# Two chunks of eight fetched by TensorE instead of one, and edge fields held in SBUF, in a graph network kernel on one Trainium2 core

## What is computed

```python
# L0, two layers: weighted messages
msg = h[src] * edge_weight[:, None]
h_neigh = segment_sum(msg, dst) * inv_deg
# L1, two layers: messages with per-edge attributes
m = (h * norm_out)[src] * (mu + exp(ls) * edge_attr)
agg = segment_sum(m, dst) * norm_in @ W + b
# L2, two layers: attention over 5 heads
e = leaky_relu(xl[src] + xr[dst]); alpha = einsum('ehc,hc->eh', e, att)
out = segment_sum(softmax_by_dst(alpha)[:, :, None] * xl[src], dst)
# L3, two layers: attention over 4 heads with 8 edge types
alpha = leaky_relu(qn[etype, dst] + kn[etype, src])
agg = segment_sum(softmax_by_dst(alpha)[:, :, None] * xw[etype, src], dst)
```

## Time and profile before

| | us |
|---|---|
| median of three runs (11,395.51 to 11,404.53) | 11,397.69 |
| the profiled execution | 11,410.16 |
| its span, first to last instruction | 11,408.1 |
| busy: DVE, PE, POOL, PEld, ACT | 6,968.2, 6,336.2, 5,957.6, 4,385.4, 1,664.8 |

### The profile page before, as it was taken

The page is one execution under the profiler, slowest core; times in us unless marked ns, Lnnn a source line. Parts: engine busy times, 40 slices in busy tenths (PEclk is TensorE's granted clock), DMA queues, the critical chain, the costliest instruction groups (busy, mean ns, idle before and its releaser), DMA issues. The chain is left out here.

```text
span 11408.1 us, 146167 instructions
## 1 busy us (share of the span) xinstructions
PE 6336.2 (56%) x31639; PEld 4385.4 (38%) x31640; DVE 6968.2 (61%) x9723; ACT 1664.8 (15%) x5751; POOL 5957.6 (52%) x6263
## 2 busy tenths in 40 slices
PE   1777777676666764555276455544743332923327
PEld 1555454444444432222166222224732221722226
DVE  6777545577767767777888677778941112711118
ACT  0222344200000001000065100004610000000000
POOL 2777677577767735666200266640007775057760
PEclk8666778666666656666555566665555555855558
DMA  2333444444444426888388388865923333333333
GB/s 66 93 91 92 111 124 126 102 122 120 116 110 122 121 64 209 261 263 263 96 350 333 124 263 262 264 189 216 388 103 87 85 85 67 98 91 85 85 78 105
DMA packets 983109, 1719.05 MB, mean 151 GB/s; under 512 B 527619, under 2 KB 597268, under 8 KB 929127
## 3 DMA queue, kind: packets, MB, share of 16 engines
q1 hardware_dynamic: 577360, 1118.77, 28.7%
q0 software_dynamic: 227424, 434.31, 17.6%
q10 hardware_dynamic: 178256, 165.14, 4.4%
HBM read 1271.04 MB, written 448.16 MB: 151 GB/s over the span
## 5 line engine op out<-in xcount | busy, mean ns | idle before, releaser
L537 POOL DMA_INDIRECT gathered_rows<-node_table,stage x2912 | 2800.0, 962 | 1245.8 <-issue 874.4
L537 POOL DMA_INDIRECT gathered_rows<-xl_table,stage x1664 | 1572.9, 945 | 1916.3 <-DMA stage<-slots 1436.6
L537 POOL DMA_INDIRECT gathered_rows<-rel_table,stage x1664 | 1570.1, 944 | 1908.4 <-DMA stage<-slots 1401.8
L557 PE MATMUL ps_sum<-messages,onehots 128*125 128x65 f32 (+3 forms) x13312 | 2209.2, 339 | 529.2 <-DVE messages L1654 246.3
L557 PEld LDWEIGHTS ps_sum<-messages,onehots 128*125 128x125 f32 x13312 | 2154.3, 254 | 660.8 <-issue 655.3
L680 PE MATMUL ps_G<-table_parts,low_onehots 125*128 125x400 bf16 x4992 | 1551.3, 486 | 818.7 <-DVE low_onehots L691 797.2
L1420 PE MATMUL ps_Z<-xr_parts,onehots_turned 125*128 x4992 | 1293.5, 437 | 1116.1 <-DVE z L1446 1067.3
L698 DVE TENSOR_TENSOR rows_by_feature<-ps_G,high_onehots 128x400 f32<-128x400 f32 x1664 | 944.3, 574 | 1159.0 <-PE ps_G L680 1126.4
L1532 PE MATMUL ps_Q<-query_parts,onehots_turned 125*128 x4992 | 655.3, 205 | 1486.9 <-DMA onehots_turned<-onehots_turned 1484.4
L1420 PEld LDWEIGHTS ps_Z<-xr_parts,onehots_turned 125*128 125x128 bf16 x4992 | 654.4, 131 | 1755.9 <-issue 1350.8
L680 PEld LDWEIGHTS ps_G<-table_parts,low_onehots 125*128 125x128 bf16 x4992 | 587.1, 128 | 1606.0 <-issue 1183.8
(11 more groups left out here) (297 smaller groups left out, 5087.8 us busy)
## 6 DMA issues: line engine op xcount, KB each, us to landing
stash_a<-gathered_rows SPq DMA_DIRECT2D x208, 1300.0 KB
kept_rows<-stash_a SPq DMA_DIRECT2D x208, 1300.0 KB
onehots<-onehots_kept SPq DMA_DIRECT2D x520, 500.0 KB
onehots_turned<-onehots_turned SPq DMA_DIRECT2D x416, 250.0 KB
stash_r<-gathered_rows ACTq DMA_DIRECT2D x208, 272.0 KB
kept_rows<-stash_r SPq DMA_DIRECT2D x208, 272.0 KB
onehots_kept<-onehots ACTq DMA_DIRECT2D x104, 500.0 KB
gathered_rows<-node_table,stage POOLq DMA_INDIRECT x2912
```

Source lines behind the costliest of these rows:

```text
L537: pool.indirect_dma_start(G[:, HALF * k + q, 0:width], None, table, bass.IndirectOffsetOnAxis(stage[:, k, field, q:q + 1], 0)).then_inc(ga ...
L557: return nc.tensor.matmul(ps_sum[0:BN, bass.ds(at, width)], S[:, j, :], M, start=False, stop=True, skip_group_check=True)
```

## The change

Five things are edited.

1. TensorE fetches two chunks of a group, and GpSimd gathers six. The table is split by the block number into a part within five (`fifth`) and a part that is summed: for each fetched chunk five one-hots (one for each position `a` in a set of five blocks) are multiplied with five tables of 64 x 5 columns, and the 15 matmuls (five times three bf16 parts) of 320 columns add up in one PSUM bank. VectorE makes ten one-hots of 128 columns in one instruction of 1,280, multiplies the bank by a one-hot of five and reduces over five, once per chunk.
2. `slots` and `stage` are gone. `src_all`, `weight_all`, `low_all`, `high_all` and `fifth_all` stay in SBUF until the fourth network needs the space; source-and-type indices and types go to DRAM once and are loaded back as a whole before the relation passes.
3. ScalarE copies the 8 index columns of a group to a small tile (`keep_index`), and in neighbour passes the 8 weight columns, from those tiles.
4. GpSimd waits itself for the slot to be free and for `keep_index`, where it waited for `stage`.
5. At the start, `types` is written with one long row per partition, where `slots` was written in pieces of 256 B; VectorE computes `fifth` and the row of the low index.

```diff
-WIDE = 16
-BANKS = D // WIDE
+FETCH = 2
+FIVE = 5
...
-        def gather_loop(pool, stage, G, width, table, field, count=HALF):
+        def keep_index(act, IDX, index, i, k):
+            nc.scalar.activation(IDX[:, k, :], index[:, bass.ds(i * U + HALF * k, HALF)], ACT.Copy).then_inc(index_kept.sem, 1)
+        def gather_loop(pool, G, width, table, IDX, free, count=HALF):
             with pool.Fori(0, TURNS) as i:
                 for k in range(K):
-                    pool.wait_ge(staged[k].sem, staged[k].at(16 * i + 16))
+                    free(pool, i, k)
+                    pool.sem_inc(pool_seen, 1)
+                    pool.wait_ge(index_kept.sem, index_kept.at(K * i + k + 1))
...
-            for t in range(BANKS):
-                pe.wait_ge(bank_picked.sem, bank_picked.at(BANKS * n + t - 1))
-                for part in range(3):
-                    last = nc.tensor.matmul(ps_G[:, t % 2, 0:WIDE * NB], OT[0:BN, k, :],
-                                            HP[:, part, WIDE * t:WIDE * (t + 1), :].rearrange("p f b -> p (f b)"),
-                                            start=part == 0, stop=part == 2)
+            for g in range(FETCH):
+                pe.wait_ge(bank_picked.sem, bank_picked.at(FETCH * n + g - 1))
+                for a in range(FIVE):
+                    for part in range(3):
+                        last = nc.tensor.matmul(ps_G[:, (FETCH * k + g) % 2, 0:D * FIVE], OT[0:BN, k, g, a, :],
+                                                HP[:, part, a, :, :].rearrange("p f b -> p (f b)"),
+                                                start=a == 0 and part == 0, stop=a == FIVE - 1 and part == 2)
...
-            v.tensor_scalar(OT[0:BN, k, :], LR[0:BN, k, :], part[0:BN, 0:1], None, ALU.is_equal).then_inc(low_made.sem, 1)
+            v.tensor_tensor(OT[0:BN, k, :, :, :], LR[0:BN, k, :].rearrange("p (g e) -> p g e", e=P).unsqueeze(2).to_broadcast([BN, FETCH, FIVE, P]),
+                            ids[0:BN, 0:FIVE].unsqueeze(1).unsqueeze(3).to_broadcast([BN, FETCH, FIVE, P]), ALU.is_equal).then_inc(low_made.sem, 1)
...
                                 ahead, slot = i + (k + K // 2) // K, (k + K // 2) % K
                                 sp.wait_ge(z_made.sem, z_made.at(4 * (K * i + k - 1)))
                                 sp.sem_inc(sp_seen, 1)
-                                sp.wait_ge(stashed[slot].sem, stashed[slot].at(16 * ahead))
-                                sp.sem_inc(sp_seen, 1)
-                                stage_next(ahead, slot)
+                                load_turned(sp, ST, ahead, slot)
```

More of the change, by code:

```diff
@@ L383, in _ @@
                     link(v.tensor_scalar(low, low, -1.0, None, ALU.add))
-                    link(v.tensor_copy(fin[:, BLOCK, :, :], be[:, 0, :].unsqueeze(2).to_broadcast([P, NT, C])))
+                    fifth = fin[:, SRC_FIFTH, :, :]
+                    link(v.tensor_scalar(fifth, high, float(FIVE), None, ALU.is_ge))
+                    for b in range(2, FIVE):
+                        link(v.scalar_tensor_tensor(fifth, high, float(FIVE * b), fifth, ALU.is_ge, ALU.add))
+                    link(v.scalar_tensor_tensor(over[:, :, :], fifth, -float(FIVE * BN), a_src, ALU.mult, ALU.add))
                     v.scalar_tensor_tensor(fin[:, SRC_TYPE, :, :], fin[:, SRC, :, :], float(R), fin[:, TYPE, :, :],
@@ L489, in build @@
         coef_made = Counted("coefficients_made")
-        staged = [Counted(f"staged_{k}") for k in range(K)]
         gathered = [Counted(f"gathered_{k}") for k in range(K)]
@@ L705, in picks_over @@
                 c.over(16 * TURNS)
-            for c in (low_made, high_made, row_picked):
+            for c in (low_made, high_made):
                 c.over(GROUPS)
-            for c in (bank_made, bank_picked):
-                c.over(BANKS * GROUPS)
+            for c in (bank_made, bank_picked, row_picked):
+                c.over(FETCH * GROUPS)
             table_split.over(1)
@@ L716, in weighted_sums @@
             with es:
-                stage = sb("stage", [P, K, R, HALF], I32, es)
-                stage_f = stage[:, :, :, :].bitcast(F32)
+                IDX = sb("index", [P, K, HALF], I32, es)
+                W = sb("weights", [P, K, HALF], F32, es)
                 G = sb("gathered_rows", [P, U, D], F32, es)
@@ L745, in _ @@
                             for k in range(K):
-                                if hist:
-                                    stage_group(sp, stage, i, k, (stashed[k],))
-                                else:
-                                    stage_group(sp, stage, i, k)
+                                if not hist:
+                                    chunks_free(sp, i, k)
                                     load_onehots(sp, S, i, k)
@@ L756, in _ @@
                     def _(pool):
-                        gather_loop(pool, stage, G, D, node_table, SRC, HALF - 1)
+                        gather_loop(pool, G, D, node_table, IDX, chunks_free, HALF - FETCH)
                     @block.scalar
                     def _(act):
+                        for k in range(K):
+                            keep_index(act, IDX, src_all, 0, k)
                         with act.Fori(0, TURNS) as i:
@@ L941, in _ @@
                         link(v.tensor_copy(ps_c[:, D:2 * D], mu))
-                        split_table(HP, BR[0:BN, :, :])
-                        pick_rows(dve, stage_f, LR, OT, HI, BR, ps_G, G, 0, 0)
+                        make_ids(ids)
+                        split_table(HP, rest[:, :, :, :])
+                        pick_rows(dve, LR, OT, HI, ids, BR, ps_G, G, 0, 0)
                         def turn(i, last_turn):
@@ L1488, in pair_scores, with relation_scores @@
                     c.over(NCH // 2)
+                index_kept.over(GROUPS + K)
                 for c in (mult_made, reduced, scored):
                     c.over(NCH // QD)
-        def relation_scores(SCORE, XQ):
+        def relation_scores(SCORE, XQ, src_type, types):
             phase[0] += 1
@@ L1537, in _ @@
                     def _(act):
+                        for k in range(K):
+                            keep_index(act, IDX, src_type, 0, k)
                         with act.Fori(0, TURNS) as i:
@@ L1713, in build @@
         segments_phase()
+        early.close()
         norm_phase()
@@ L1860, in build, with _ @@
             dense(H[:, :, :], D, [wfc[:, :]], take, None, after)
+        kept_types = sb("kept_types", [P, 2, NS], I32)
+        types_back = sem("types_back")
+        with nc.Block() as block:
+            @block.sync
+            def _(sp):
+                sp.dma_start(kept_types[:, :, :], types_dram).then_inc(types_back, 16)
+                sp.wait_ge(types_back, 16)
         norm_phase()
```

221 lines of the change are left out of this document (123 added, 98 removed).

## The result

The changed kernel takes 11,659.4 us (median; 11,658.1 to 11,661.7) against 11,396.6 us (11,391.8 to 11,404.5) for the kernel before: a ratio of 1.023, 95% interval 1.0212 to 1.0248. The profiled execution has a span of 11,659.9 us, 251.8 more than before; the medians differ by 262.8, because the profiled execution of the kernel before took 13.6 us more than its median and that of the changed kernel 2.3. The prediction was 11,726 us: the sign and the main mechanism hold, and one term of its sum, the gain in the pair passes, was half as large as it should have been.

The account below looks back on a forecast made before the run. It took GpSimd's gathers to bound most passes, a VectorE-TensorE loop the first neighbour and attribute passes, and `stage` waits to slow pair passes. 374 + 212 - 130 - 120 - 8 = +328 us gave 11,726 us, range 11,440 to 11,960.

Parts of the forecast that it names:

- the gain in the pair passes: Pair passes with `stage` gone: between -128 and 0 us per pass, taken as -60, so -120 us for both.
- The loop in three passes: First neighbour and attribute passes: VectorE and TensorE wait for each other in a loop; +212 and +374 us.
- The fixed part: Loop time per group besides the fetch F: 4.7 us in an attribute pass, 5.06 in the first neighbour pass.
- The fetch: TensorE's 30 matmuls per group: 4.35 us at a high clock, 8.1 at a low one, 6.1 expected.
- d: Time into a fetch after which TensorE's clock rises: taken as 3.4 us; the range counted 2.9 to 4.8.
- The second neighbour pass: Loop open there, one-hots ready ahead, so the pass falls to GpSimd's six gathers, 7.49 us per group: -130 us.
- the other reading: Pair passes: DMA engines go round queues packet by packet, so gathers get their share during a store; both passes -256 us.
- second rival: Pair passes at GpSimd's pace, the rest as forecast: 136 us less, 11,590 us; chance 0.12.
- The rest: Start of the kernel and starts of pair and relation passes: -13, +4, +5 and 4 x -1, -8 us.
- The break-even: Where the first rival's outcome changes sign: F + 4.7 near 9.9 us, a fetch of 5.2 us.
- first rival: TensorE's clock stays high in all four neighbour and attribute passes: -218 us, 11,180 us; chance 0.13.
- The rival in which the change doesn't do what it says: Gathers are issued, but their waits, with ScalarE's index copy queued, hold GpSimd; folded into the range, no chance of its own.

Follow-up runs that it names:

- ahead: The changed kernel with VectorE making a group's one-hots one group earlier, same instructions: 10,582 us, 0.9286 of the kernel before (12,737 us on the slow chip).
- hold_clock: The changed kernel with 12 more matmuls per group, useless for the output, in TensorE's pause in the two attribute passes: 11,276 us in one run.
- pair_seven: The changed kernel with seven gathers instead of eight per group in the pair passes, leaving out every eighth chunk's scores: 11,394 us in one run.
- the first four runs: Changed kernel, slow chip: old one-chunk fetch 13,365 us; one chunk by five one-hots 13,209; two chunks only in second neighbour pass 13,133; one-hots a group earlier 12,737.
- run 50: Not a run's number: "that run" is the first measurement of `ahead`, on the slow chip, 12,737 us; 50 counts its late gathers in a pair pass.

## Why the prediction was right, and where it was not

- **The loop in three passes** was the mechanism. `ahead` shows it by opening the loop, `hold_clock` by shortening one term of it. The fixed part was 4.9 us in an attribute pass where the prediction had 4.7: in the group shown the pick starts 0.11 us behind the fetch instead of 0.04, and from the end of the reduce to the next one-hots it is 2.15 us instead of 2.05, with 0.03 in the other links. Attribute passes +383 (forecast +374), first neighbour pass +227 (+212).
- **The fetch**: 1.48 us for the one-hots and 0.49 for a pick came out as the slope of the earlier trace rows gave them. The reduce took 0.49; the forecast has 0.47, where the slope that it names gives 0.50. The fetch at a high clock took 4.25 us against 4.35; the other bound, 8.1, was never reached (the longest took 7.2), so it and its allowance for the last matmul remain untested. The mean fetch of the attribute passes is 6.1 us, as forecast, and in the shown group of 5.92 the clock is low for about the 3.4 us that the prediction chose as d. That choice was a judgment between 2.9 and 4.8, which would have made some 75 us less or 205 more, and in part luck: the reason given for it (no waits for picks) was not tested, and the low stretch does not begin where it was thought to.
- **The second neighbour pass**: -129 us, forecast -130.
- **The pair passes are the step that failed.** From the earlier trace rows (421 GB/s in the store, 201 outside it) the prediction concluded that gathers and stores take turns rather than overlap, and took half of the possible gain, -60 us per pass. It was -126 and -124. What the prediction set beside it as the other reading, that gathers get their share during a store, gives -256; the runs gave -251, with 310 GB/s during the store and 296 behind it. The mean tells it: 7.4 us at 0.74 and 3.2 at 1.08 are a share of 0.84, and the same bytes in 10.0 instead of 11.2 us need no more than 0.94; in the trace after they needed 0.88, 292 GB/s. The burst of 421 GB/s followed a long stretch at 201, so it shows what the engines can carry, not that a group's bytes need all of it. `pair_seven` shows the room left at 10.0 us: 314 GB/s at 8.74. The bound to compute is the bytes of a group over the rate that was shown to be possible: 201 GB/s for 7.4 us and 421 for 3.2 us are 2.8 MB, 6.7 us at 421 GB/s, far under GpSimd's 10.0. This was the prediction's second rival, 11,590 us, to which it gave 0.12. The measured time lies between it and the forecast because the other terms went the other way (+15 and +9 in the passes of the loop, +1, and +29 for the rest), and 11 us are the difference of the profiled executions from the medians. So the total is only 67 us off where this term alone was 131 off: errors of other signs hid half of it.
- **The rest** was forecast at -8 and came to +21. The start gained 14.5 us, where 13 less 4 were forecast; what was left out is the drain: when GpSimd is through, the last groups still run round the loop, and a slower loop makes this longer too (+18.4 us behind the first neighbour pass, +5.9 and +7.0 behind the attribute passes).
- **The break-even** of the first rival is a little off: by the prediction's own terms the losses and gains meet at 9.75 us per group, a fetch of about 5.05 us, not 9.9 and 5.2. Nothing else hangs on it.
- The rival in which the change doesn't do what it says did not occur: GpSimd waits for ScalarE's index copy only at the start of a pass.

## What to carry to other kernels

Before work is moved from a busy engine to idle ones, follow the dependency round once: idle engines with a closed loop between them have no time to give. The cure may be to start a link of that loop one round earlier, which takes up one more slot of a buffer and no instruction (here the slot was there): it turned +2.3% into -7.1%. Where engines wait for each other, the price of TensorE's work contains its clock: with a pause of 3 us in each group a fetch cost 40 to 70% more here (5.9 to 7.1 us instead of 4.25). And before a burst in a trace is taken for a full resource, divide the bytes of a whole period by the highest rate seen.

## What the runs showed of the hardware

- TensorE with more to do can be sooner done: 12 useless matmuls per group in its pause (1.79 us) shortened the fetch that followed from 6.1 to 4.3 us in the mean, and the attribute passes by 370 us together.
- The low clock need not begin in the pause: in the group shown it was 1.00 through a pause of 3.1 us and fell 0.7 us after the fetch had begun.
- A VectorE comparison with both inputs in SBUF holds up a gather that GpSimd is issuing: 0.94 us became up to 1.9 beside them, 1.029 us in the mean of that pass; with one input read from PSUM, 0.944.
- One chip was slower than the others. On the one of the first four runs, the time of the kernel before was 13,536 us (13,480 to 13,580). GpSimd's gathers took 0.94 us there too, but in the first relation pass of `ahead`, with 26 turns of its loop, 28 of the 831 spacings from one gather to the next were 6 us and more instead of 1.25, and nothing that the profile shows was waited for, as in this row:

```profile
10034.57 0.94 POOL L553 DMA_INDIRECT gathered_rows<-rel_table,index  x1 [6.80 <-issue]
```

In a pair pass of that run 50 gathers, every sixteenth from the fortieth on, came 8.6 to 10.8 us after the one before, mostly 10.4. What it is was not settled; no edit of these kernels was aimed at it.
